# Wide attention in a decoder kernel: row sums spread over a head's partitions, values scaled before one output product

## What is computed

```python
q = query @ w_q;  k, v = split(context @ w_kv)          # heads of 64
scores = einsum('bhqd,bhkd->bhqk', q, k) * 64 ** -0.5
attn = softmax(scores, axis=-1)
out = einsum('bhqk,bhkd->bhqd', attn, v)
x = x + out.reshape(B, NQ, 1024) @ w_out + b_out        # w_out: 1024 x 128
```

## Time and profile before

| | |
|---|---|
| median of 3 runs | 4416.5 us (4411.14 to 4419.23) |
| profiled execution, its own time | 4420.43 us |
| its span | 4418.3 us |
| TensorE busy | 3788.1 us, 86% |
| VectorE busy | 2793.8 us, 63% |
| ScalarE busy | 1988.5 us, 45% |
| GpSimd busy | 1809.8 us, 41% |
| the wide attention's steps | 2103 to 4171 us |

### The profile page before, as it was taken

One profiled execution on the slowest core, in us unless ns is written; L12 is line 12 of the kernel. 1 busy time (PEld: TensorE's weight loads), 2 busy tenths in 40 slices (PEclk: granted clock), 3 DMA queues, 4 the chain that ended last, 5 costly groups with the idle time before them and its releaser, 6 DMA issues. The chain is left out here.

```text
span 4418.3 us, 57485 instructions
## 1 busy us (share of the span) xinstructions
PE 3788.1 (86%) x22136; PEld 1586.3 (36%) x22136; DVE 2793.8 (63%) x4384; ACT 1988.5 (45%) x2249; POOL 1809.8 (41%) x728
## 2 busy tenths in 40 slices
PE   5674478888888879875999999999999999999889
PEld 1222112222122234332444444444444444444443
DVE  4336899999999503367666666666666666665232
ACT  2441067777777863340444344444444444444311
POOL 3500000000000000230777777777778777778700
PEclk7885599999999989775999999999999999999889
DMA  2004000100100010240000000000001001001010
GB/s 61 15 8 93 6 1 1 27 1 3 25 1 1 1 41 0 76 182 0 24 26 27 27 27 27 28 28 25 27 26 30 25 26 29 24 27 31 23 56 5
DMA packets 71846, 122.95 MB, mean 28 GB/s; under 512 B 9741, under 2 KB 25691, under 8 KB 70907
## 3 DMA queue, kind: packets, MB, share of 16 engines
q1 hardware_dynamic: 71580, 119.28, 9.6%
HBM read 84.62 MB, written 34.64 MB: 27 GB/s over the span
## 5 line engine op out<-in xcount | busy, mean ns | idle before, releaser
L950 POOL TENSOR_TENSOR att_total<-att_total,att_prob 128x1024 f32<-128x1024 f32 x608 | 1569.6, 2582 | 453.9 <-ACT att_prob L1138 403.5
L1153 DVE TENSOR_REDUCE att_top_piece<-PS 128x1 f32<-128x512 f32 (+1 forms) x1664 | 1037.4, 665 | 405.7 <-PE PS L1006 397.1
L1138 ACT ACTIVATE att_prob<-PS 128x1024 f32<-128x1024 f32 x816 | 791.2, 1022 | 1087.1 <-PE PS L1072 1087.1
L544 DVE TENSOR_REDUCE att_top_piece<-PS 128x1 f32<-128x512 f32 (+4 forms) x1856 | 1128.7, 654 | 221.7 <-PE PS L421 110.6
L525 ACT ACTIVATE att_prob<-PS 128x1024 f32<-128x1024 f32 x912 | 880.5, 1021 | 359.2 <-PE PS L460 293.8
L1085 PE MATMUL PS<-att_prob,att_vals 128*64 128x512 f32 x3264 | 792.7, 605 | 6.7 <-ACT att_prob L1138 6.7
L421 PE MATMUL PS<-cross_Kstack,cross_Qstack 64*128 64x512 bf16 (+1 forms) x1664 | 343.3, 403 | 277.4 <-DVE att_top_piece L544 256.6
L1006 PE MATMUL PS<-att_k_hi,att_q_hi 64*128 64x512 f32 (+1 forms) x1664 | 399.6, 472 | 105.6 <-DVE att_top_piece L1153 77.1
L479 PE MATMUL PS<-att_prob,cross_Vst 128*32 128x512 f32 x3264 | 438.3, 606 | 0.6 <-ACT att_prob L525 0.4
L361 POOL COPY cross_Vst<-cross_Vall 128x1836 f32<-128x1836 f32 x4 | 7.6, 1908 | 1041.2 <-PE PS L479 993.2
L421 PEld LDWEIGHTS PS<-cross_Kstack,cross_Qstack 64*128 64x128 bf16 x1664 | 94.9, 94 | 788.2 <-DVE att_top_piece L544 750.1
(11 more groups left out here) (239 smaller groups left out, 2938.8 us busy)
## 6 DMA issues: line engine op xcount, KB each, us to landing
att_vals<-values SPq DMA_DIRECT2D x192, 256.0 KB, 2.6
values<-mla_stage SPq DMA_DIRECT2D x24, 1024.0 KB, 4.1
f_w<-in_f_w SPq DMA_DIRECT2D x40, 256.0 KB, 4.3
cross_Kstack<-kparts SPq DMA_DIRECT2D x36, 204.0 KB
kparts<-proj_parts SPq DMA_DIRECT2D x42, 128.0 KB
att_vals<-values SPq DMA_DIRECT2D x16, 192.0 KB, 2.4
k_ctxT<-in_ctxT SPq DMA_DIRECT2D x1, 2448.0 KB
cross_Kstack<-kparts SPq DMA_DIRECT2D x36, 64.0 KB
```

Source lines behind the costliest of these rows:

```text
L544: dve.tensor_reduce(top_piece[:, n % 2, k, c:c + 1], PS[:, bank(p + s), 0:w], AX, ALU.max).then_inc(dve_freed, 1)
L950: pool.tensor_tensor(so_far, so_far, prob[0:rows, j % RING, :, :], ALU.add).then_inc(summed, 1)
L1138: act.activation(prob[:, j % RING, :, :].rearrange("p a b -> p (a b)"), PSf[:, b:b + 2 * HALF], ACT.Exp, scale=scale).then_inc(exped, 1)
L1153: dve.tensor_reduce(top_piece[:, n % 2, s * QT + qt, c:c + 1], PS[:, bank(at + s), 0:w], AX, ALU.max).then_inc(dve_freed, 1)
```

## The change

- GpSimd adds `total_dve` into `total` when a unit ends (`fold`). `s` moves to kt 7 of the next unit and is two products of 64 columns of ones (weights) with `total` (512 columns): every partition of a head then holds that head's sums, in one bank. ScalarE copies them to `sums`.
- VectorE inverts `sums` in four slices of 128 columns, at kt 11, 15, 19, 23. GpSimd multiplies `outU` by them at kt 25 (`scale_out`).
- `y` moves to kt 30: 4 products over all 128 partitions, one bank, and one VectorE addition of 128x512 to x.
- The places of `q` (kt 20 before) and of odd units' `k` (kt 1, 7, ... before) move; in odd units the late `m` of the pair at kt 1 and 2 goes between the last weighted product of the old unit and the first of the new.
- The loads of `wo` and of the output bias move in SyncE's queue; the bias goes to a part of `top`.

```diff
+    S_AT, SLICES, SCALE_AT, Y_AT = 7, (11, 15, 19, 23), 25, 30
-        if n >= 1 and kt == 3:
+        if n >= 1 and kt == S_AT:
             items.append(("s", n - 1))
-        if n >= 1 and kt == 5:
+        if n >= 1 and kt == Y_AT:
             items.append(("y", n - 1))
-        if kt == 20 and n + 2 < UNITS:
+        if kt == (18 if n % HALVES == 0 else 34) and n + 2 < UNITS:
             items.append(("q", n + 2))
-        f = (kt - 3) // 6 if n % HALVES == 0 else 8 + (kt - 1) // 6
+        f = (kt - 3) // 6 + (0 if n % HALVES == 0 else 8)
+        if p + 1 < PAIRS and kt < 49 and kt % 6 == 3 and f < KF:
...
+            def fold(n):
+                pool.wait_ge(summed, sum_count[n * KT + KT - 1])
+                pool.wait_ge(dve_summed, dve_sums[n])
+                pool.tensor_tensor(total[:, n % 2, :, :], total[:, n % 2, :, :], total_dve, ALU.add).then_inc(folded, 1)
+            def scale_out(n):
+                pool.wait_ge(inverted, (n + 1) * len(SLICES))
+                pool.wait_ge(out_copied, n + 1)
+                pool.tensor_tensor(outU[:, n % 2, :], outU[:, n % 2, :], sums[:, :], ALU.mult).then_inc(scaled, 1)
...
-                    if f == 5 and n % HALVES == 0 and 1 < p - 1 < PAIRS:
+                    if f == 10 and n % HALVES == 0 and 1 < p - 1 < PAIRS:
+                        sp.wait_ge(side_filled, filled_count[("y", n - 1)])
                         load_out(p - 1)
+            sp.wait_ge(side_filled, filled_count[("t", UNITS - 1)])
+            sp.dma_start(bo, A["x1_bo"]).then_inc(bo_loaded, 16)
...
+                    pe.wait_ge(folded, n + 1)
                     for s in range(2):
-                        for qt in range(QT):
-                            k = s * QT + qt
-                            pe.matmul(PS[:, bank(at), k:k + 1], total[:, n % 2, s, qt * P:(qt + 1) * P],
-                                      ones_col[:, :], start=True, stop=False)
-                            ins = pe.matmul(PS[:, bank(at), k:k + 1], total_dve[:, s, qt * P:(qt + 1) * P],
-                                            ones_col[:, :], start=False, stop=True)
+                        ins = pe.matmul(PS[strip(s), bank(at), :], ones_wide[:, :], total[:, n % 2, s, :],
+                                        start=True, stop=True, tile_position=(0, s * DH2))
...
+                    pe.wait_ge(scaled, n + 1)
                     for qt in range(QT):
-                        for s in range(2):
-                            ins = pe.matmul(PS[:, bank(at + s), qt * D:(qt + 1) * D],
-                                            outU[strip(s), n % 2, qt * P:(qt + 1) * P],
-                                            wo[strip(s), n // HALVES % 2, :], start=True, stop=True,
-                                            tile_position=(s * DH2, 0))
+                        ins = pe.matmul(PS[:, bank(at), qt * D:(qt + 1) * D], outU[:, n % 2, qt * P:(qt + 1) * P],
+                                        wo[:, n // HALVES % 2, :], start=True, stop=True)
...
+                between = j >= 2 and (j - 1) % KT == 0
                 if j >= 2:
                     weigh(j - 2)
+                    if between:
+                        for item in late[j // 2]:
+                            side(item)
                     weigh(j - 1)
-                for item in whole[j // 2] + late[j // 2]:
+                for item in whole[j // 2] + ([] if between else late[j // 2]):
                     side(item)
...
+                elif kind == "s":
+                    if n >= 1:
+                        act.wait_ge(scaled, n)
+                    act.activation(sums[:, :], PS[:, bank(at), :], ACT.Copy).then_inc(negated, 1)
...
+                    rows = flat(x[:, n % HALVES * QT:(n % HALVES + 1) * QT, :])
+                    dve.tensor_tensor(rows, rows, PS[:, bank(at), :], ALU.add).then_inc(dve_freed, 1)
+            def invert(n, i):
+                dve.wait_ge(negated, negated_count[("s", n)])
+                piece = slice(i * HALF // len(SLICES), (i + 1) * HALF // len(SLICES))
+                dve.reciprocal(sums[:, piece], sums[:, piece]).then_inc(inverted, 1)
```

More of the change, by code:

```diff
@@ L841, in attend_wide_heads @@
             turned += 1
-        if n >= 1 and kt == 3:
+        if n >= 1 and kt == S_AT:
             items.append(("s", n - 1))
-        if n >= 1 and kt == 5:
+        if n >= 1 and kt == Y_AT:
             items.append(("y", n - 1))
-        if kt == 20 and n + 2 < UNITS:
+        if kt == (18 if n % HALVES == 0 else 34) and n + 2 < UNITS:
             items.append(("q", n + 2))
-        f = (kt - 3) // 6 if n % HALVES == 0 else 8 + (kt - 1) // 6
-        if p + 1 < PAIRS and kt == (6 * f + 3 if n % HALVES == 0 else 6 * (f - 8) + 1) and 0 <= f < KF:
+        f = (kt - 3) // 6 + (0 if n % HALVES == 0 else 8)
+        if p + 1 < PAIRS and kt < 49 and kt % 6 == 3 and f < KF:
             items.append(("k", p + 1, f))
@@ L862, in attend_wide_heads @@
         place[item] = len(freed)
-        if item[0] in ("m", "y"):
+        if item[0] == "m":
             freed += [("dve", len(dve_count) + 1), ("dve", len(dve_count) + 2)]
             dve_count[item + (0,)], dve_count[item + (1,)] = len(dve_count) + 1, len(dve_count) + 2
-        elif item[0] == "t":
+        elif item[0] in ("t", "s"):
             negated_count[item] = len(negated_count) + 1
@@ L883, in attend_wide_heads @@
         sum_count.append(by_dve if dve_adds(j) else by_pool)
-    pool_sums = [len([j for j in range((n + 1) * KT) if not dve_adds(j)]) for n in range(UNITS)]
     dve_sums = [len([j for j in range((n + 1) * KT) if dve_adds(j)]) for n in range(UNITS)]
@@ L905, in attend_wide_heads @@
         wk, wq = m.sb("wk", [DC, 2, P]), m.sb("wq", [P, 2, P])
-        wo, bo, ones_col = m.sb("wo", [P, 2, D]), m.sb("bo", [1, D]), m.sb("ones_col", [P, 1])
+        wo, ones_wide = m.sb("wo", [P, 2, D]), m.sb("ones_wide", [P, DH2])
         prob, total = m.sb("prob", [P, RING, 2, HALF]), m.sb("total", [P, 2, 2, HALF])
         top_piece, top = m.sb("top_piece", [P, 2, 2 * QT, MF]), m.sb("top", [P, QT, P])
+        bo = top[0:1, 0, :]
         total_dve = flat(xn[:, :, :]).rearrange("p (s q) -> p s q", s=2)
-        inv = m.sb("inv", [P, 2 * QT])
+        sums = m.sb("sums", [P, HALF])
         outU = O[:, :, :].rearrange("p (u t) d -> p u (t d)", u=2)
@@ L919, in attend_wide_heads @@
         summed, dve_summed = m.sem("summed"), m.sem("dve_summed")
-        out_copied, added = m.sem("out_copied"), m.sem("added")
+        folded, inverted, scaled, out_copied = m.sem("folded"), m.sem("inverted"), m.sem("scaled"), m.sem("out_copied")
         bias_summed, bias_added = m.sem("bias_summed"), m.sem("bias_added")
@@ L936, in _ @@
                 pool.wait_ge(ones_set, 2 * g + 4)
-            pool.memset(ones_col[:, :], 1.0).then_inc(ones_set, 1)
+            pool.memset(ones_wide[:, :], 1.0).then_inc(ones_set, 1)
+            def fold(n):
[6 more added lines that the diff above has]
+                pool.tensor_tensor(outU[:, n % 2, :], outU[:, n % 2, :], sums[:, :], ALU.mult).then_inc(scaled, 1)
             for j in range(STEPS):
                 n, kt = j // KT, j % KT
+                if kt == SCALE_AT and n >= 1:
+                    scale_out(n - 1)
                 if kt == 0 or dve_adds(j):
@@ L950, in _ @@
                     pool.tensor_tensor(so_far, so_far, prob[0:rows, j % RING, :, :], ALU.add).then_inc(summed, 1)
+                if kt == KT - 1:
+                    fold(n)
+            scale_out(UNITS - 1)
         @block.sync
@@ L965, in _ @@
                 load_out(p)
-            sp.dma_start(bo[:, :], A["x1_bo"]).then_inc(bo_loaded, 16)
             for n in range(UNITS):
@@ L993, in side @@
                 wait_place(at)
-                if kind in ("m", "y"):
+                if kind == "m":
                     wait_place(at + 1)
-                if kind == "m":
                     c, qt = item[2:]
@@ L1026, in side @@
                 elif kind == "s":
-                    pe.wait_ge(summed, pool_sums[n])
-                    pe.wait_ge(dve_summed, dve_sums[n])
+                    pe.wait_ge(folded, n + 1)
                     for s in range(2):
-                        for qt in range(QT):
-                            k = s * QT + qt
-                            pe.matmul(PS[:, bank(at), k:k + 1], total[:, n % 2, s, qt * P:(qt + 1) * P],
-                                      ones_col[:, :], start=True, stop=False)
-                            ins = pe.matmul(PS[:, bank(at), k:k + 1], total_dve[:, s, qt * P:(qt + 1) * P],
-                                            ones_col[:, :], start=False, stop=True)
+                        ins = pe.matmul(PS[strip(s), bank(at), :], ones_wide[:, :], total[:, n % 2, s, :],
+                                        start=True, stop=True, tile_position=(0, s * DH2))
                 else:
-                    pe.wait_ge(out_copied, n + 1)
+                    pe.wait_ge(scaled, n + 1)
```

(35 more changed lines are left out.)

## The result

The changed kernel takes 4340.1 us at the median of 4 runs (4337.0 to 4347.6). The kernel before, with one more run, is at 4417.9. The ratio is 0.9825, 95% interval 0.9803 to 0.9848: 1.75% or 77 us faster. Forecast were 4344 us, from 4328 to 4370. The profiled execution took 4342.9 us, 77.6 less than the one before; the forecast's sum for that was -72.0.

The account below looks back on a forecast made before the run. TensorE was taken to bound the kernel, GpSimd the end. -80.4 (`s`, `y`) + 8.7 (`q`, `k` parted) - 2.5 (`m`) + 2.2 (end) = -72.0 us: profiled 4420.4 to 4348.4, median forecast 4344 us, range 4328 to 4370.

Parts of the forecast that it names:

- The path: Wide attention: ScalarE's pairs of exponentials always wait for TensorE, whose time for a pair of steps sets the length.
- Removed work: Units 1 to 14: excess of pairs with old `s` 73.1 us and old `y` 36.8 us, together 109.9 us.
- The clock's 23 us: Old `s` pairs: the cost beyond 3.6 us of products at full clock, put down to TensorE's lowered clock, 23 us.
- New products: New `s` and `y` on TensorE: 0.93 and 1.18 us a unit, each at most 1.63; 29.5 us over 14 units.
- Parting `q` and `k`: Pairs with `q` and `k`: 11.94 us apart against 11.32 before, losing 0.62 us a unit, +8.7 us; bounds 0 to 8.7.
- The `m` in the gap: Odd units: an `m` fills part of the first weighted product's 0.84 us wait for the copy, -2.5 us over seven units.
- Work beside TensorE: ScalarE's copy, VectorE's reciprocals, GpSimd's fold and scaling: hidden, costed at nothing; the reciprocals uncovered would be 53 us.
- Unit 15 and the end: Last unit: GpSimd sets the end; additions end at 114.9 us, 17.5 us follow; together +2.2 us, bounds -3 and +7.
- The clock rival: TensorE's clock falls anyway, from something at the unit's start: 23 us come back, 4367 us; chance 0.08.
- The reciprocals' rival: VectorE's reciprocals don't hide and hold TensorE up: all 56 uncovered give +53 us, 4397 us; chance 0.07.
- GpSimd as the bound: GpSimd's additions at 3.31 us throughout would set the units' length: +24 us, 4441 us; chance 0.03.
- The range's lower end: 4328 us: below the forecast, -2.4 from the whole 0.84 us gap, -4 from `y` at its least, -9 if `q` alone stalls nothing.

Follow-up runs that it names:

- experiment 3: Kernel before, with 64 moving columns of ones instead of one in each of the 16 products of `s`: 4390.5 us, ratio 0.9941.
- experiment 6: Changed kernel with `q` back in one pair with `k`, at kt 21 in all units: median 4333.5 us, ratio 0.9796 to the kernel before.
- experiment 8: Changed kernel with the late `m` of odd units behind both weighted products again: pair at kt 1 5.41 us against 5.20, one execution.
- experiments 4 and 2: 4: changed kernel without the reciprocals, 4340.3 us. 2: kernel before with only GpSimd's fold, `s` of 8 one-column products, 4370.5 us, ratio 0.9886.
- experiment 5: Changed kernel with one reciprocal of 128x512 a unit at kt 11 instead of four slices: 4361.6 us, ratio 0.9864 to the kernel before.
- experiment 7: Changed kernel with VectorE taking every odd kt from 7 to 47 in unit 15: 4335.4 us, ratio 0.9807 to the kernel before.
- experiment 1: Kernel before with only the places of `s`, `y`, `q`, `k` and the loads changed, old forms kept: 4430.6 us, ratio 1.0022.

## Why the prediction was right, step by step

**The path.** Right: TensorE's length of a pair set the time in units 1 to 14, before and after, and the changes of the pairs with `s`, `y`, `q` and `k` make up 78.0 us there (forecast -80.4 + 8.1 - 2.5, one `q` lying in unit 0: -74.8).

**Removed work.** Right: the excess of 73.1 and 36.8 us is gone from the old places; nothing was given back elsewhere. The clock's 23 us of it was inferred from rates; experiment 3 shows it as 22.3.

**New products.** Right, with each forecast a little high: `s` adds 5.20 - 4.34 = 0.86 (forecast 0.93), `y` 5.45 - 4.34 = 1.11 (1.18), 1.9 us over 14 units. That neither stalls as `k` does (1.63) holds.

**Parting `q` and `k`.** Right: 11.94 us in both pairs, and experiment 6 returns it.

**The `m` in the gap.** Right in sign, too large: -2.5 us forecast, 1.5 by experiment 8. TensorE's timeline of the changed kernel shows the gap filled as intended:

```profile
2483.30 1.08 PE L1099 MATMUL PS<-att_prob,att_vals 128*64 128x512 f32 x4
2484.30 0.49 PE L1028 MATMUL PS<-att_k_hi,att_q_hi 64*128 64x512 f32 x2
...
2485.21 1.08 PE L1099 MATMUL PS<-att_prob,att_vals 128*64 128x512 f32 x4 [0.41 <-issue]
```

The weighted product still starts 1.91 us behind the one before it, with the `m` inside. Of its 0.33 us only 0.21 came off the pair, and the timelines show where the rest stays. Whatever stands first behind the second weighted product takes 0.33 to 0.34 us to the next start: the `m` in experiment 8, the first score product now, while the next one takes 0.24.

```profile
2486.22 0.51 PE L1073 MATMUL PS<-att_q_hi,att_k_hi 64*128 64x512 f32 x2
2486.56 0.40 PE L1073 MATMUL PS<-att_q_lo,att_k_hi 64*128 64x512 f32 x2
2486.80 0.40 PE L1073 MATMUL PS<-att_q_hi,att_k_lo 64*128 64x512 f32 x2
```

**Work beside TensorE.** Right: experiments 4 and 2 show the reciprocals and the fold hidden. What the argument didn't give is the margin, which experiment 5 measures.

**Unit 15 and the end.** Right: the additions end 115.8 us behind the first pair (forecast 114.9) and 17.0 us follow (17.5): +2.5 against +2.2. Most of the 0.9 is GpSimd's scaling, 2.26 us in unit 15 where 1.3 was taken; its median over the units is 1.29. Experiment 7 shows what sets the end, GpSimd's queue, which the forecast left as a loss and which is worth 9.6 us once work leaves that queue.

**The rivals.** The clock rival fell: after the change the clock is 1.00 over units 1 to 14, and experiment 3 ties its fall to the products with one moving column. The reciprocals' rival fell for slices and holds for one operation. GpSimd as the bound fell in units 1 to 14, where no exponential of ScalarE waits for it, and holds in unit 15 alone. Of the 5.6 us by which the profiled executions beat the sum, 3.2 lie in units 1 to 14; the rest is in stretches that the change doesn't touch (-2.2 together) and in the small differences of unit 0 and unit 15.

**Slips in the working.** The range's lower end takes 2.4 us for the whole 0.84 us gap; 7 x 0.84 less the 2.5 already counted is 3.4. The length of a unit, 131.6 us, is counted from GpSimd's additions; the starts of the units give 131.2 (1836.2 over 14). Neither moves the forecast.

## What to carry to other kernels

Read the cost of a small item from the length of the loop step that holds it, not from its own busy time: here 3.6 us of products cost up to 6.8. A reduction over partitions by products with a single column should have the large operand moving and the ones as weights, which also leaves the result where the next elementwise operation wants it. Work that goes to an in-order engine beside the path hides only in pieces shorter than that engine's room in a step (experiment 5), and the last unit, where the loop's other work is missing, needs a split of its own.

## What the runs showed of the hardware

- The granted clock of TensorE fell from 2.4 to 1.2 GHz in a busy burst. 16 products of a 128x128 load and one moving column run without idle time. They take 3.6 us where the clock stays at 1.00; in other units it falls among them, to 0.50, and the last products take 0.43 us each instead of 0.22 (experiment 1). With 64 moving columns, the same loads and the same 0.227 us each, it stayed at 1.00 in every unit (experiment 3). The Trainium skill (TensorE: Matmul & The Clock Gate, "Part 1: The HAM clock gate") ties the low clock to idleness. The trace differs: at 0.50 TensorE's rows fill 5.00 of 5 us.
- A reciprocal of 128x128 takes 0.94 us among other work, four in a row 3.39, one of 128x512 3.34: nearly by the element, with no gain from one instruction. None of them was drawn out, though GpSimd is busy for 83% of units 1 to 14: they took 0.89 to 0.95 us (64 of them, changed kernel) and 3.34 to 3.35 (16, experiment 5).
